# Three more groups' sums turned by VectorE in blocks, and a one-hot moved ahead of each block turn

## The chip, the cores and the metric

The kernel runs on one core of a Trainium2 chip. TensorE (matmuls), VectorE, ScalarE and GpSimd each work through their own queue of instructions in order, and SyncE issues most of the DMAs; between the queues only semaphores order the work. The metric is the device time of one execution in microseconds (us). The profile calls the engines PE (PEld for its weight loads), DVE, ACT, POOL and SP; "q" behind a name is the engine's sequencer.

## The reference

Two graph layers on 1250 nodes of 512 features, with 40000 edges (source, destination, a 512-wide attribute each), sorted by destination:

```
h = relu(layernorm(x))
msg = (h[src] + edge_attr) @ Wm.T + bm
agg = segment_sum(msg, dst) / max(degree, 1)
x1  = x + layernorm(h + gelu(concat(h, agg) @ Wu.T + bu)) * gamma + beta
h1  = relu(layernorm(x1))
rst = (1 + eps) * h1 + segment_sum(h1[src], dst)
out = x1 + relu(rst @ W1 + b1) @ W2 + b2 + h1
```

The kernel sums first and multiplies afterwards: it needs the sum of the edge attributes for each destination (a 1250 x 512 table, kept transposed in `aggT`) and a matrix of counts, how often each source node occurs for each destination (`A16`, 16 bit). With the counts, both sums over `h[src]` become dense matmuls.

## The kernel before

**Groups.** The edges are read in NG = 79 groups of 512, group n by one DMA of 1 MB into buffer n % 4 of `ea` (`sync`, L351 to L357). As destinations are sorted, half a group touches at most W = 22 neighbouring nodes. One step n of the main loop on each engine stands for group n.

**Sums.** `sums(n)` (L1170) is TensorE's work for group n: matmuls with the one-hot `oneD` of destinations as the weights and the edge data moving. VectorE makes that one-hot in `sums_hots(n)` (L725, the instruction is on L729), three groups ahead. The sums come out with destinations on the partitions and must be turned before they can be added to `aggT`. There are two ways, and `EARLY` divides them:

- Groups below EARLY: `sums` writes 8 matmuls of 256 columns (L1185; each is two records in the trace). ScalarE copies them out (`packed_copy`, L512), TensorE turns them with two transposes (`turn`, L1208, the instruction on L1213), ScalarE copies again (`turned_copy`, L518), and GpSimd adds both halves to `aggT` (L445).
- Groups from EARLY on: `sums` writes 16 matmuls of 128 columns (L1193), laid out so that a transposition within blocks of 32 x 32 is enough. VectorE does it straight out of TensorE's memory (`turn_blocks`, L762, the instruction on L768), and adds both halves itself (`add_sums_of`, L770, the instruction on L779). `sums(n)` for n of at least EARLY + 2 waits until `turn_blocks(n - 2)` is done, since both write the same bank (L1177).

**Counts.** The counts are made ahead: `counts(m)` (L1197) on TensorE and `add_counts(m, half)` (L754, L760) on VectorE are done for up to two groups m a step, so that group 78 is counted at step FULL = 58. Step 57 has groups 76 and 77, step 58 has group 78. EARLY is FULL + 1 = 59.

**The handover.** From step 60 on TensorE has one or, from step 64, pairs of "pieces": `piece(i)` (L1276, matmuls on L1295 and L1296) multiplies the 512 x 128 block of `h` in two parts (`Hh`, `Hl`) with a block of the counts. From step 64 the loop takes steps in pairs, both `sums` first. Piece 0 needs all counts added, the block converted by ScalarE (`piece_conv`, L562), the bank free that VectorE empties in `bias_out` (L783, tile `cbB`), and `Hl` from VectorE (`low_h0`, L794), which in turn needs `Hh` from ScalarE (`high_h0`, L551). `high_h0(0)` waits for the bias product (L1149) at the end of TensorE's step 58.

**VectorE's order.** Its program is the loop at L867. In a step n from 60 to 66 it issues: `turn_blocks(n - 1)`, the loading of that group's offsets into registers, `sums_hots(n + 2)`, the two additions of group n - 1, `low_h0(n - 58)`, and one `fold` (L804), a 16-bit addition over 1280 elements toward the degrees. Step 58 has the counts of group 78 and `low_h0(0)`; step 59 has `bias_out`, `low_h0(1)` and two folds; step 67 has a maximum over the degrees (L917) in place of the fold. At step OUT_AT = 70 VectorE waits for piece 9 before it goes on. After the loop TensorE goes on with the update (L1401), the second layer's counts (L1377, L1378) and the two dense layers (L1454, L1470).

Of the kernel before, what the change touches and what calls it, by code (L numbers as in the profile page):

```python
# [18 lines left out]
SUM_HOTS = 3  # L19
# [11 lines left out]
def gnn_kernel(nc, x, src, dst, edge, Wm, bm, Wu, bu, gamma, beta, W1, b1, W2, b2, eps, out):  # L31
# [9 lines left out]
    NG = -(-E // GE)  # L41
    ETAIL = E - (NG - 1) * GE
    GP = NG + 1
    HB = NT
# [7 lines left out]
    NX = NP // XW  # L52
    WU_ORDER = list(range(FC, 2 * FC)) + list(range(FC))
    assert ETAIL % 2 == 0 and ETAIL <= GE // 2 and D == GE and FC == 4 and sum(n for _, n in QS) == NP
    assert len(QS) == 3 and QS[2][1] * 2 == 512 and KW <= 256 and NT == 10

# [5 lines left out]
    FULL = COUNTED.index(NG)  # L62
# [15 lines left out]
    assert all(T_AT[b] + 2 <= U_AT[b][0] for b in range(NT)) and GEN_AT not in ASIDE  # L78

    WARM = 5  # L80
    EARLY = FULL + 1
    FOLD_AT = [EARLY] + list(range(EARLY, EARLY + HB - 2))
    CONV_AT = FULL + 1
    PIECE_AT = FULL + 2
    DEG_AT = FOLD_AT[-1] + 2
    DEG_PARTS = [range(0, NT // 2), range(NT // 2, NT)]
# [4 lines left out]
    IN_LOOP = NG - PIECE_AT  # L91
    assert IN_LOOP <= 2 * NT and HAS_AT[-1] < NG and DEG_AT + 4 < HAS_AT[0] and len(FOLD_AT) == HB - 1
    assert len(BIAS_AT) == NT and all(BIAS_AT[b] <= HAS_AT[b] for b in range(NT))
    PAIRS_FROM = PIECE_AT + 4
    PAIRED = [[n] for n in range(PAIRS_FROM)] + [[n for n in (k, k + 1) if n < NG] for k in range(PAIRS_FROM, NG, 2)]
    assert PAIRS_FROM > max(EARLY, GEN_AT) and [OUT_AT, OUT_AT + 1] in PAIRED
    DEG_BANK = 2
# [119 lines left out]
    with ctx:  # L217
# [198 lines left out]
        def _(pool):  # L416
# [16 lines left out]
            def add_sums_of(n):  # L433
                _, loaded = nc.values_load_multi_w_load_instructions(
                    offrow[0:1, n * 4:n * 4 + 2].bitcast(I32), engines=(mybir.EngineType.Pool,), min_val=0, max_val=(NP << 16) - 1,
                    skip_runtime_bounds_check_because="a pair of least indices of nodes")
                for half, first in enumerate((loaded[0] & 0xFFFF, loaded[0] >> 16)):
                    first = nc.s_assert_within(first, 0, NP - 1, skip_runtime_bounds_check_because="each is the least of indices of nodes")
                    cols = aggT[:, :, bass.ds(first, W)]
                    if half == 0:  # L440
                        pool.wait_ge(turned_out, n + 1)
                    if n > 0 or half > 0:
                        pool.wait_ge(early_step, n * 2 + half)
                    sums = turned_sums[n % TURNS][:].rearrange("p (f q) -> p f q", f=FC)[:, :, half * QUAD:half * QUAD + W]
                    nc.gpsimd.tensor_tensor(cols, sums, cols, ALU.add).then_inc(early_step, 1)  # L445

            pool.wait_ge(offs_in, 16)
            pool.wait_ge(sums_zero, 1)
            for n in range(EARLY):
                add_sums_of(n)  # L450
# [26 lines left out]
        def _(act):  # L477
# [30 lines left out]
            def packed_copy(n):  # L508
                act.wait_ge(sums_done, n + 1)
                if n >= TURNS:  # L510
                    act.wait_ge(turned, n - TURNS + 1)
                nc.scalar.copy(packed_sums[n % TURNS][:], ps[:, n % 2, 0:D // 2]).then_inc(packed_out, 1)  # L512

            def turned_copy(n):
                act.wait_ge(turned, n + 1)
                if n >= TURNS:
                    act.wait_ge(early_step, (n - TURNS + 1) * 2)
                nc.scalar.copy(turned_sums[n % TURNS][:], ps[:, 2 + n % 2, 0:D // 2]).then_inc(turned_out, 1)  # L518
# [14 lines left out]
            def bias_parts_out():  # L533
                act.wait_ge(bm_mm, 1)
                nc.scalar.copy(bm_parts[:], ps[:, ASIDE_BANK["product", FC], :]).then_inc(bm_out, 1)
# [34 lines left out]
            for n in range(NG):  # L570
# [3 lines left out]
                if n - 1 == BIAS_PRODUCT_AT[0]:  # L574
                    bias_parts_out()
                if n < EARLY:
                    packed_copy(n)
                if 0 < n <= EARLY:
                    turned_copy(n - 1)
# [27 lines left out]
            large = act.value_load(most1[0:1, 0:1], min_val=0, max_val=E + P)  # L607
            act.wait_ge(sum_step, 2 * (NG - EARLY))
            act.wait_ge(piece_mm, 2 * NT)
# [68 lines left out]
        def _(dve):  # L678
# [46 lines left out]
            def sums_hots(n):  # L725
                if n >= SUM_HOTS:
                    dve.wait_ge(sums_done, n - SUM_HOTS + 1)
                n1 = idxT["srel"][:, :, n:n + 1].broadcast_to([P, SUB, W])
                V.tensor_tensor(oneD[n % SUM_HOTS][:], iotaF[:, 0:W].rearrange("p (a n) -> p a n", a=1).broadcast_to([P, SUB, W]), n1,  # L729
                                ALU.is_equal).then_inc(hotD_ready, 1)  # L730
# [16 lines left out]
            def offsets(n):  # L747
                _, loaded = nc.values_load_multi_w_load_instructions(
                    offrow[0:1, n * 4:n * 4 + 2].bitcast(I32), engines=(mybir.EngineType.DVE,), min_val=0, max_val=(NP << 16) - 1,
                    skip_runtime_bounds_check_because="a pair of least indices of nodes")  # L750
                return [nc.s_assert_within(first, 0, NP - 1, skip_runtime_bounds_check_because="each is the least of indices of nodes")
                        for first in (loaded[0] & 0xFFFF, loaded[0] >> 16)]
# [9 lines left out]
            def turn_blocks(n):  # L762
                dve.wait_ge(sums_done, n + 1)
                if n < TURNS + EARLY:
                    dve.wait_ge(early_step, (n - TURNS + 1) * 2)
                else:
                    dve.wait_ge(sum_step, (n - TURNS + 1 - EARLY) * 2)
                V.transpose(turned_sums[n % TURNS][:], ps[:, n % 2, 0:D // 2]).then_inc(blocks_turned, 1)  # L768
# [27 lines left out]
            def fold(c):  # L796
                if c > 1:
                    dve.wait_ge(fold_step, c - 1)
                here = A16[:, c, 0:NP]
                if c == 1:  # L800
                    dve.wait_ge(add_step, 2 * NG)
                    dve.wait_ge(u1_mm, NT)
                before = A16[:, 0, 0:NP] if c == 1 else acc[:]
                V.tensor_tensor(Dsum[:] if c == HB - 1 else acc[:], before, here, ALU.add).then_inc(fold_step, 1)  # L804
# [60 lines left out]

            count_first, sum_first = offsets(0), None
            for n in range(NG):  # L867
                if n > EARLY:
                    turn_blocks(n - 1)
                    sum_first = offsets(n - 1)  # L870
                if n > 0 and n - 1 + SUM_HOTS < NG:
                    sums_hots(n - 1 + SUM_HOTS)
                for m in COUNTS[n]:
                    first = count_first
                    add_counts(m, 0, first[0])
# [36 lines left out]
                for c in range(1, HB):  # L912
                    if FOLD_AT[c - 1] == n:
                        fold(c)
                if n == FOLD_AT[-1] + 1:
                    dve.wait_ge(fold_step, HB - 1)
# [190 lines left out]
        def _(pe):  # L1107
# [323 lines left out]
            for _, b in filler:  # L1431
                last = times_A(b, "B")
# [66 lines left out]
```

## Time and profile before

| what | value |
|---|---|
| three executions | median 483.59 us (482.88 to 483.61) |
| the profiled execution | 483.73 us; its span, from the first to the last instruction, 481.9 us |
| TensorE busy | 468.1 us (97% of the span) |
| VectorE busy | 260.6 us (54%) |
| ScalarE, GpSimd busy | 172.0 us (36%), 123.3 us (26%) |
| chain that ended last, by engine | PE 89%, DVE 3%, issue 3%, DMA 2%, all else 1% or less each |
| granted TensorE clock | 1.00 of full speed all through |

The page counts an engine as busy while an instruction of its kind is under way; ends of matmuls are modelled, so the distance from one start to the next tells more than a duration. "Idle before" is the time in which the engine stood still ahead of an instruction, with the instruction that the profile holds to have ended it. The chain that ended last is followed back from the last instruction, at each step to what released it.

### The profile page before, as it was taken

The page shows a single profiled execution, that of the slowest core. Times are in us where ns is not written, and L with a number is a line of the kernel's source. Part 1 is how long each engine was busy: PE and PEld are TensorE (multiplying, and loading weights), DVE is VectorE, ACT ScalarE, POOL GpSimd, SP SyncE. Part 2 cuts the span into 40 slices and gives each one's busy share as a digit, 9 for nine tenths or more (in the row PEclk, how much of TensorE's full clock was granted, in tenths as well). Part 3 has the DMA queues.
Part 4 walks back from the last instruction along what each step waited for, and adds up shares of the span by engine and source line. Part 5 has one row for each costly group of instructions (what it writes and reads, how often), then busy time and mean ns, then how long its engine had stood idle before and what let it go on. Part 6 is the DMA issues. An engine that isn't in the chain of part 4 may idle for free.

```text
span 481.9 us, 9420 instructions
## 1 busy us (share of the span) xinstructions
PE 468.1 (97%) x3313; PEld 282.3 (59%) x3313; DVE 260.6 (54%) x615; ACT 172.0 (36%) x332; POOL 123.3 (26%) x185
## 2 busy tenths in 40 slices
PE   6999999999999999999999999899999999999997
PEld 5555555454555455788765755799744449444445
DVE  4799887778787877997847599822000000011011
ACT  6677642333333337521049387920021213000000
POOL 4016434443343422000000232449980000000000
PEclk9999999999999999999999999999999999999999
DMA  8999999999999999999430111030220000010111
GB/s 280 377 395 407 409 387 387 406 389 403 394 387 402 407 396 382 345 347 339 167 89 22 44 45 40 28 148 1 74 101 0 0 0 1 22 44 23 44 44 38
DMA packets 31832, 98.92 MB, mean 205 GB/s; under 512 B 3686, under 2 KB 4906, under 8 KB 31786
## 3 DMA queue, kind: packets, MB, share of 16 engines
q1 hardware_dynamic: 30570, 97.27, 53.4%
q10 hardware_dynamic: 1216, 1.05, 0.7%
q8 instruction: 27, 0.44, 0.4%
q14 instruction: 19, 0.16, 0.1%
HBM read 95.76 MB, written 2.56 MB: 204 GB/s over the span
## 4 chain that ended last, share of the span: by engine, by line
PE 89%; DVE 3%; issue 3%; DMA 2%; DVEq 1%; ACT 1%; SPq 0%; POOL 0%; ACTq 0%; POOLq 0%
PE ps L1470 14%; PE ps L1454 14%; PE ps L1185 11%; PE ps L1401 7%; PE ps L1234 7%; PE ps L1204 6%; PE ps L1377 4%; PE ps L1378 4%; PE ps L1295 4%; PE ps L1213 4%; PE ps L1296 4%; PE ps L1193 3%; PE ps L1137 3%; DMA WmN<-in_L_gnn_Wm_dram 2%; DVE A L760 1%
## 5 line engine op out<-in xcount | busy, mean ns | idle before, releaser
L445 POOL TENSOR_TENSOR aggT<-turned_sums,aggT 128x88 f32 x118 | 61.3, 520 | 96.7 <-ACT turned_sums L518 83.7
L760 DVE TENSOR_TENSOR A<-ps,A 128x220 f32 x158 | 60.8, 385 | 33.0 <-PE ps L1204 24.1
L1098 DVE TENSOR_TENSOR U<-ps,U 128x512 f32<-128x512 f32 x9 | 6.2, 692 | 122.3 <-PE ps L1470 122.3
L1470 PE MATMUL ps<-W2s,hid 128*128 128x512 f32 (+1 forms) x176 | 68.9, 553 | 0.0
L1454 PE MATMUL ps<-aggT,W1s 128*128 (+1 forms) x192 | 67.3, 513 | 0.0
L1185 PE MATMUL ps<-ea,oneD 128*22 128x256 f32 x944 | 62.6, 383 | 3.1 <-issue 2.8
L1454 PEld LDWEIGHTS ps<-aggT,W1s 128*128 128x128 f32 x192 | 36.4, 190 | 30.7 <-issue 30.6
L1470 PEld LDWEIGHTS ps<-W2s,hid 128*128 128x128 f32 (+1 forms) x176 | 32.6, 185 | 36.0 <-issue 34.5
L1185 PEld LDWEIGHTS ps<-ea,oneD 128*22 128x22 f32 x944 | 23.3, 101 | 50.0 <-issue 25.3
L512 ACT COPY packed_sums<-ps 128x256 f32<-128x256 f32 x59 | 22.0, 372 | 80.7 <-PE ps L1185 80.5
L1377 PE MATMUL ps<-AR,Hh 128*128 128x256 f32 (+2 forms) x160 | 43.8, 310 | 0.0
L1378 PE MATMUL ps<-AR,Hl 128*128 128x256 f32 (+2 forms) x160 | 43.0, 305 | 0.0
L739 DVE TENSOR_TENSOR oneK<-iotaP,P_key 128x1760 bf16<-128x1760 bf16 (+1 forms) x40 | 42.6, 1064 | 0.0
L669 ACT ACTIVATE hid<-ps,b1C 128x512 f32 (+1 forms) x24 | 14.6, 608 | 77.7 <-PE ps L1454 77.7
L1204 PE MATMUL ps<-oneK,oneS 128*128 128x220 bf16 x316 | 40.9, 260 | 0.4 <-DVE A L760 0.4
L1234 PE MATMUL ps<-Wu1T,U 128*128 128x512 f32 x80 | 41.3, 598 | 0.0
L1401 PE MATMUL ps<-CT,aggT 128*128 128x512 f32 x80 | 35.5, 592 | 0.0
L1295 PE MATMUL ps<-ARc,Hh 128*128 128x512 f32 x80 | 32.8, 410 | 0.7 <-DVE Hl L794 0.7
L1204 PEld LDWEIGHTS ps<-oneK,oneS 128*128 128x128 bf16 x316 | 29.9, 97 | 2.8 <-issue 1.0
L1296 PE MATMUL ps<-ARc,Hl 128*128 128x512 f32 x80 | 31.6, 394 | 0.0
L1378 PEld LDWEIGHTS ps<-AR,Hl 128*128 128x128 f32 x160 | 30.2, 189 | 1.7
L1377 PEld LDWEIGHTS ps<-AR,Hh 128*128 128x128 f32 x160 | 30.2, 189 | 1.6
(152 smaller groups left out, 631.5 us busy)
## 6 DMA issues: line engine op xcount, KB each, us to landing
ea<-in_edge_attr_dram SPq DMA_DIRECT2D x78, 1024.0 KB, 8.7
X<-in_x_dram SPq DMA_DIRECT2D x1, 2304.0 KB
xt<-in_x_dram SPq DMA_DIRECT2D x9, 256.0 KB, 2.5
out_dram<-U SPq DMA_DIRECT2D x9, 256.0 KB
W1s<-in_L_gnn_W_dram SPq DMA_DIRECT2D x1, 2048.0 KB, 9.0
W2s<-in_L_gnn_W_dram SPq DMA_DIRECT2D x1, 2048.0 KB, 8.4
Wu2N<-in_L_gnn_Wu_dram ACTq DMA_DIRECT2D x2, 512.0 KB, 4.2
WmN<-in_L_gnn_Wm_dram SPq DMA_DIRECT2D x1, 1024.0 KB, 7.3
```

The costliest lines, as they stand in the source:

```text
L445: nc.gpsimd.tensor_tensor(cols, sums, cols, ALU.add).then_inc(early_step, 1)
L760: V.tensor_tensor(cols, ps[:, 4 + m % 2, half * KW:(half + 1) * KW].rearrange("p (h w) -> p h w", w=W), cols, ALU.add).then_inc(add_step, 1)
L1185: last = T.matmul(to.rearrange("p (c d) -> p c d", c=2), oneD[h][:, g * 2 + j, :], data, start=j == 0, stop=j == 1)
L1204: last = T.matmul(ps[:, 4 + m % 2, (j // 2) * KW:(j // 2 + 1) * KW], sources[:, j // 2, :, j % 2], keys[:, j // 2, :, j % 2], start=j % 2 ...
L1234: quarter = T.matmul(ps[:, ASIDE_BANK["u1", b], :], U[:, b, f * P:(f + 1) * P], Wu1T[:, f, :], start=f == 0, stop=f == FC - 1)
L1295: T.matmul(to, Hh[:, c, rows], here, start=c == 0 and (q < 2 or f % 2 == 0), stop=False)
L1296: last = T.matmul(to, Hl[:, c, rows], here, start=False, stop=c == NT - 1 and (q < 2 or f % 2 == 1))
L1377: T.matmul(to, Hh[:, b, rows], AR[:, b, start:start + cols], start=b == 0 and (cols == 512 or f % 2 == 0), stop=False)
L1378: last = T.matmul(to, Hl[:, b, rows], AR[:, b, start:start + cols], start=False, stop=b == NT - 1 and (cols == 512 or f % 2 == 1))
L1401: last = T.matmul(ps[:, 2 + b % 2, :], aggT[:, f, b * P:(b + 1) * P], CT[:, f, :], start=f == 0, stop=f == FC - 1)
L1454: last = T.matmul(ps[:, CHUNK_BANK[k % 4], 0:cols], W1s[:, f, k * P:(k + 1) * P], aggT[:, f, bass.ds(start, cols)], start=f == 0, stop=f = ...
L1470: last = T.matmul(ps[0:rows, Y_BANK[b + half], 0:cols.stop - cols.start], hid[:, k, b * P:b * P + rows], W2s[:, k, cols], start=k == 0, st ...
```

## The change

Two things are changed. EARLY becomes FULL - 2 = 56, so groups 56, 57 and 58 go by VectorE's block turning and not by ScalarE, TensorE's transposes and GpSimd; FOLD_AT is written with FULL so that it stays [59, 59, 60, ..., 66]. And in VectorE's loop `sums_hots` stands ahead of `turn_blocks` and the loading of offsets, for every step from 57 on.

```
-    EARLY = FULL + 1
-    FOLD_AT = [EARLY] + list(range(EARLY, EARLY + HB - 2))
+    EARLY = FULL - 2
+    FOLD_AT = [FULL + 1] + list(range(FULL + 1, FULL + HB - 1))
...
             for n in range(NG):
+                if n > 0 and n - 1 + SUM_HOTS < NG:
+                    sums_hots(n - 1 + SUM_HOTS)
                 if n > EARLY:
                     turn_blocks(n - 1)
                     sum_first = offsets(n - 1)
-                if n > 0 and n - 1 + SUM_HOTS < NG:
-                    sums_hots(n - 1 + SUM_HOTS)
                 for m in COUNTS[n]:
```

## Rows read from the trace of the kernel before

**Rows 1.** All waits of engine PE from 172 to 250 us: total us, times, longest us

```profile
PE ps L1295 <- DVE Hl L794: 0.7, 1, 0.7
PE ps L1193 <- DVE oneD L729: 0.2, 1, 0.2
```

**Rows 2.** Timeline of PE, steps 58 to 61: start us, us, engine, line, operation

```profile
181.75 1.05 PE L1185 MATMUL ps<-ea,oneD 128*22 128x256 f32 x16
182.73 0.44 PE L1213 MATMUL ps<-ident,packed_sums 128*128 128x128 f32 x2
183.00 0.56 PE L1204 MATMUL ps<-oneK,oneS 128*128 128x220 bf16 x4
...
184.37 1.07 PE L1193 MATMUL ps<-ea,oneD 128*22 128x128 f32 x32
185.37 0.44 PE L1213 MATMUL ps<-ident,packed_sums 128*128 128x128 f32 x2
185.74 1.07 PE L1193 MATMUL ps<-ea,oneD 128*22 128x128 f32 x32
187.51 0.47 PE L1295 MATMUL ps<-ARc,Hh 128*128 128x512 f32 x1 [0.70 <-DVE Hl L794]
...
189.75 1.07 PE L1193 MATMUL ps<-ea,oneD 128*22 128x128 f32 x32
```

**Rows 3.** Timeline of DVE, steps 58 to 60; idle before and its releaser in brackets

```profile
183.78 0.39 DVE L760 TENSOR_TENSOR A<-ps,A 128x220 f32 x1 [0.67 <-PE ps L1204]
184.34 0.39 DVE L760 TENSOR_TENSOR A<-ps,A 128x220 f32 x1 [0.18 <-DVE A L760]
185.12 0.69 DVE L794 TENSOR_TENSOR Hl<-X,Hh 128x512 fp32r<-128x512 f32 x1 [0.39 <-ACT Hh L551]
185.73 0.24 DVE L729 TENSOR_TENSOR oneD<-iotaF,T_srel 128x88 f32<-128x88 f32 x1
185.89 0.68 DVE L783 COPY cbB<-ps 128x512 f32<-128x512 f32 x1
186.77 0.69 DVE L794 TENSOR_TENSOR Hl<-X,Hh 128x512 fp32r<-128x512 f32 x1 [0.19 <-ACT Hh L551]
187.38 1.00 DVE L804 TENSOR_TENSOR acc<-A 128x1280 uint16<-128x1280 uint16 x1
188.41 0.83 DVE L804 TENSOR_TENSOR acc<-acc,A 128x1280 uint16<-128x1280 uint16 x1
189.15 0.44 DVE L768 STREAM_TRANSPOSE turned_sums<-ps 128x256 f32<-128x256 f32 x1
189.52 0.21 DVE L729 TENSOR_TENSOR oneD<-iotaF,T_srel 128x88 f32<-128x88 f32 x1
189.81 0.25 DVE L779 TENSOR_TENSOR aggT<-turned_sums,aggT 128x88 f32 x1
190.24 0.25 DVE L779 TENSOR_TENSOR aggT<-turned_sums,aggT 128x88 f32 x1 [0.18 <-DVE aggT L779]
190.41 0.69 DVE L794 TENSOR_TENSOR Hl<-X,Hh 128x512 fp32r<-128x512 f32 x1
```

**Rows 4.** Timeline of PE, the sums of group 65 and of groups 68 and 69

```profile
200.21 1.07 PE L1193 MATMUL ps<-ea,oneD 128*22 128x128 f32 x32 [0.20 <-DVE oneD L729]
...
210.95 2.00 PE L1193 MATMUL ps<-ea,oneD 128*22 128x128 f32 x64
```

**Rows 5.** Timeline of DVE, the block turns of groups 67 and 77

```profile
211.29 0.44 DVE L768 STREAM_TRANSPOSE turned_sums<-ps 128x256 f32<-128x256 f32 x1
...
240.16 0.44 DVE L768 STREAM_TRANSPOSE turned_sums<-ps 128x256 f32<-128x256 f32 x1
240.82 0.25 DVE L779 TENSOR_TENSOR aggT<-turned_sums,aggT 128x88 f32 x1 [0.21 <-DVE turned_sums L768]
```

**Rows 6.** Timeline of ACT, the second copy of group 58's sums

```profile
185.84 0.37 ACT L518 COPY turned_sums<-ps 128x256 f32<-128x256 f32 x1 [0.75 <-PE ps L1213]
```

**Rows 7.** Timeline of POOL, the last addition of group 58

```profile
187.03 0.67 POOL L445 TENSOR_TENSOR aggT<-turned_sums,aggT 128x88 f32 x1 [0.21 <-POOL aggT L445]
```

## The prediction

> **What bounds the kernel now.** I read the page first: TensorE is busy 97% of the span and makes up 89% of the chain that ended last, so a microsecond off TensorE's queue is worth one, provided that nothing else is late in its place. So the next view is where TensorE waits around the change. From 172 to 250 us the profile knows two waits, both ended by VectorE [rows 1]: 0.7 us ahead of piece 0, and 0.2 us ahead of the sums of group 65 [rows 2, 4]. No DMA is among them. The third view is VectorE's timeline at the same place [rows 3]. In steps 59 to 61 it hardly stands still, and TensorE goes by it: the block turn of group 59 starts at 189.15 and is reported for 0.44, and the sums of group 61, which wait for it by the code, start at 189.75, that is 0.60 after the turn's start. The same distance recurs twice. The turn of group 67 starts at 211.29, so sums 69 may start at 211.89; sums 68 start at 210.95 and the pair takes 2.00 where one group takes 1.07, so TensorE itself is there 0.93 later, at 211.88 [rows 4, 5]. The two are level there, and the 2.00 us for the pair is all work. Between 185 and 212 us VectorE is thus as late as TensorE, or later; only step 70, at which it waits for piece 9 by the code, takes it off the path. From there on the chain is TensorE's nearly without a break.
>
> **The change part by part.**
>
> *Three transposes leave TensorE.* One takes 0.27 us from its start to the next work (182.73 to 183.00) and the last, in step 59, takes 0.37 (185.37 to 185.74): 0.91 us in all. The sums cost the same in both layouts, 0.98 against 1.00 us (181.75 to 182.73, 184.37 to 185.37) [rows 2]. If nothing else were late, this is what the change brings: -0.9 us.
>
> *Six copies leave ScalarE, six additions leave GpSimd.* Nobody waits for these engines here, with one exception: `Hh` of block 1 stands behind the copy at 185.84, which waits for TensorE's last transpose [rows 6], and VectorE idles 0.19 for that `Hh` [rows 3]. It goes.
>
> *Three block turns and six additions come to VectorE.* The prices are in [rows 3]. The next instruction starts some 0.08 before the reported end of the one before it (a turn 0.37, an `Hl` 0.61). From a turn's start to the first addition it is 0.66, to the second 0.43 more, to the next instruction 0.17 more. In steps 57 and 58 this is covered. VectorE idles 0.67 ahead of the counts of group 78 at 183.78, and TensorE delivers these 0.54 earlier, since it is two transposes ahead. The additions of group 56 (0.43 + 0.17), a one-hot (0.16) and the turn of 57 (0.37) make 1.13 us; the one-hot was there before, so 0.97 are new, against 1.21 us of cover less some latency. I let the second count addition start at 184.3, as before. Then follow the additions of group 57 (184.6 and 185.0), and `Hl` of block 0 at 185.15: it was at 185.12 because of an idle 0.39 for its `Hh`, which now comes 0.54 earlier. Up to here the change costs nothing, and this is the last cover.
>
> *Then it costs.* From 185.15: one-hot +0.61 = 185.76; turn of 58 +0.16 = 185.92; additions +0.66 = 186.58 and +0.43 = 187.01; `cbB` +0.17 = 187.18 (before 185.89); `Hl` of block 1 +0.60 = 187.78 (186.77); the first fold +0.61 = 188.39; the second +1.03 = 189.42; one-hot +0.74 = 190.16; turn of 59 +0.16 = 190.32, where it was at 189.15. VectorE is 1.17 us later. What TensorE makes of it: sums 60 may start 0.60 after the turn of 58, at 186.5 and not 185.74. Behind this wait stand sums 60 and everything TensorE has. Piece 0 waits for `cbB` (187.18 + 0.68 + 0.16 = 188.0, before 187.51) and its 2.06 us of work end at 190.1 (187.51 to 189.75 less the wait of about 0.2). Sums 61 wait for the turn of 59: 190.32 + 0.60 = 190.9, against 189.75. The whole saving is used up and 1.17 us are lost.
>
> *The one-hot ahead of the turn, on every step.* Before, the one-hot stood between the turn and the first addition and cost nothing: with it the addition starts 0.66 after the turn (189.15 to 189.81) [rows 3], and without any one-hot there, for group 77, it is 0.66 as well (240.16 to 240.82) [rows 5], since the addition waits for the turn's result. Ahead of the turn it has nothing to hide behind. Its price there isn't in the trace. The nearest rows: from a one-hot to a copy that doesn't depend on it 0.16 (185.73 to 185.89), which I take; from a one-hot to a waiting addition 0.29 (189.52 to 189.81) as the upper end; 0, if the turn's start is set by something else, as the lower. From step 61 to 68 there are 8 more of them, so the turn of 67 is later by 1.17 + 8 x 0.16 = 2.45 us. TensorE was level with it, so sums 69 start 2.45 us later: of this it meets 1.8 at sums 65 (1.17 + 4 x 0.16; the row at 200.21 shows that it waits there) and the rest at sums 69.
>
> *GpSimd beside the folds.* GpSimd's last addition runs from 187.03 to 187.70 and is long [rows 7]; the first fold, begun at 187.38, takes 1.00 us where the second takes 0.83 [rows 3]. With GpSimd done before step 59 I let the first fold lose this: 1.03 becomes 0.85, -0.18 us. The ends are 0 (the fold's own form, it alone reads two blocks of `A16`) and -0.18. The Trainium skill, SBUF — State Buffer, section "Who interferes with whom", says that a VectorE instruction with two inputs in SBUF contends with a GpSimd instruction that reads SBUF, and that whoever starts first holds the shared ports to the end. By that rule the 0.18 is all GpSimd's and the sum is 2.27; without it, if the form sets the fold's time, it is 2.45. The rows fit the rule, but two instructions don't prove it.
>
> *Afterwards.* At step 70 VectorE waits for piece 9 and so comes back into step with TensorE. From step 71 on it has 0.16 more a step, against about a microsecond of slack or more that I take from TensorE's having no wait on it up to 250 us [rows 1]. The later stages all begin with TensorE's or VectorE's last results of the loop, so I pass the loss on in full.
>
> The sum: 1.17 + 1.28 - 0.18 = +2.27 us on the profiled execution's 483.73 us, 486.0 us. That execution lies 0.14 above the median of the three runs, so a median would be near 485.9, which I give.
>
> **The rivals.**
>
> *The one-hot hides after all (0 in place of 0.16 for each of nine).* Then the loss is 2.27 - 9 x 0.16 = +0.8 us, 484.4. For it: the sequencer also loads offsets and handles waits between the instructions, and may set the turn's start anyway. Against it: in steps 60 to 66 the turn starts 0.74 after a fold of 0.83, directly behind it [rows 3], so it is VectorE's own work that sets its start.
>
> *The one-hot costs more (0.29).* Then 2.27 + 9 x 0.13 = +3.4 us, 487.1. For it: the turn has two semaphores to wait for and the copy at 185.89 one.
>
> *TensorE's saving arrives: not slower.* One mechanism: VectorE's new work of step 59 (turn and additions of 58, 1.26 us) finds cover, so that the turn of 59 is in time for piece 0's end. It decides at the turn of 59: it would have to start at 189.15 less 0.9, or 188.3, 2.0 us earlier than I work out. If so the time is 483.6 - 0.9 = 482.7. Against it: every interval in the row of instructions above is one that [rows 3] show without idle time.
>
> *The loss is given back later*, in a wait of TensorE behind 250 us that has a fixed time of its own. The issue share of the chain (3%) is the room for it. Then it is between 484 and 485.
>
> **How the numbers follow.** The forecast, 485.9, with its own range of 484.9 to 486.9, has 0.62. The hidden one-hot has 0.12, the dearer one 0.10, the saving 0.06, the loss given back 0.10. The range that should hold 8 times in 10 leaves out the saving and part of the two others: 484.2 to 487.1. About 0.2% (0.97 us) is what a measurement of this kernel can tell from no change. Faster by more needs the saving and a little luck: 0.04. Within 0.2%, up to 484.56: the hidden one-hot, most of the saving, half of what is given back, 0.18. Slower: 0.78.
>
> **What would show it.** TensorE's timeline should have no L1213 after 177 us, sums 58 at 181.5, and new idle time ahead of sums 60 and 61, ended by VectorE. VectorE's should have turns at 183.3, 185.9 and 190.1 for groups 57 to 59, one-hots straight ahead of each, the turn of group 67 at 213.6, and a first fold of 0.83. The wait at sums 65 should be near 1 us, with a further one at sums 69 of about half a microsecond. If sums 61 start at 190.9 or 190.7 and the end isn't later, the loss was given back behind 250 us. If the turns of 59 and 67 stay 22.14 us apart (211.29 less 189.15), the one-hot is hidden and my 1.28 is wrong. If sums 60 start before 186, the cover of step 58 was larger than I saw.

## The result and the profile after

The changed kernel takes 487.20 us, median of six runs (487.03 to 488.61), against 483.65 us (482.88 to 483.82) before, also six: a ratio of 1.0077, with an interval of 1.0067 to 1.0088. It is slower, as forecast, but by 3.6 us and not by 2.3, and lies just outside the range that ended at 487.1.

The head of the page of the changed kernel, and its chain that ended last by engine:

```profile
span 486.1 us, 9495 instructions
PE 468.8 (96%) x3355; PEld 284.1 (58%) x3355; DVE 262.9 (54%) x624; ACT 169.9 (35%) x326; POOL 120.6 (25%) x179
PE 86%; DVE 6%; issue 4%; DMA 2%; DVEq 2%; ACT 0%; SPq 0%; POOL 0%; ACTq 0%; POOLq 0%
```

VectorE makes up 6% of the chain where it had 3%. This profiled execution took 488.61 us, the longest of the six, and it was already 1.69 us behind the kernel before at 81 us of the span, a stretch in which nothing is changed. A second profile of the same kernel (e4 below) shows no such lead-in: at 81 us it is 0.08 behind. I read the change from that one. Its end is not typical either: its span is 485.4 us where the median is 484.7, because the last output's DMA ended 2.16 us after VectorE's last instruction, and 1.40 before. So I compare starts of instructions in it, and spans by medians. All waits of TensorE from 172 to 250 us in it, where before there were 0.7 and 0.2 us [rows 1]:

```profile
PE ps L1193 <- DVE turned_sums L768: 3.3, 4, 1.6
PE ps L1295 <- issue: 0.6, 1, 0.6
```

The four waits are seen one by one in TensorE's timeline of e4 (start us, us, engine, line, operation, idle time before it and who ended it):

```profile
184.01 1.07 PE L1193 MATMUL ps<-ea,oneD 128*22 128x128 f32 x32
186.67 1.07 PE L1193 MATMUL ps<-ea,oneD 128*22 128x128 f32 x32 [1.59 <-DVE turned_sums L768]
188.37 0.47 PE L1295 MATMUL ps<-ARc,Hh 128*128 128x512 f32 x1 [0.63 <-issue]
...
191.13 1.21 PE L1193 MATMUL ps<-ea,oneD 128*22 128x128 f32 x32 [0.65 <-DVE turned_sums L768]
...
202.13 1.07 PE L1193 MATMUL ps<-ea,oneD 128*22 128x128 f32 x32 [0.59 <-DVE turned_sums L768]
...
214.44 1.07 PE L1193 MATMUL ps<-ea,oneD 128*22 128x128 f32 x32 [0.51 <-DVE turned_sums L768]
```

These are sums 59, sums 60, piece 0 and sums 61, 65 and 69. (For piece 0 the profile names no releaser; by the code it needs the bank that VectorE's copy to `cbB` empties, and it starts 0.10 after that copy's reported end.) Sums 59 start 0.36 earlier than before (184.01 against 184.37), so the transposes' time really is saved on TensorE. Sums 60 start 0.93 later (185.74 before), sums 61 1.38 later (189.75), sums 65 1.92 later (200.21), sums 69 2.56 later (214.44 against 211.88) [rows 2, 4]. TensorE's last matmul is 2.56 us later too: what is lost by sums 69 is lost for good.

VectorE's timeline of e4 over the same steps, to be laid beside [rows 3]:

```profile
184.43 0.39 DVE L760 TENSOR_TENSOR A<-ps,A 128x220 f32 x1 [0.18 <-DVE A L760]
...
185.32 0.68 DVE L794 TENSOR_TENSOR Hl<-X,Hh 128x512 fp32r<-128x512 f32 x1
185.92 0.24 DVE L729 TENSOR_TENSOR oneD<-iotaF,T_srel 128x88 f32<-128x88 f32 x1
186.08 0.44 DVE L768 STREAM_TRANSPOSE turned_sums<-ps 128x256 f32<-128x256 f32 x1
186.74 0.25 DVE L779 TENSOR_TENSOR aggT<-turned_sums,aggT 128x88 f32 x1 [0.21 <-DVE turned_sums L768]
187.17 0.26 DVE L779 TENSOR_TENSOR aggT<-turned_sums,aggT 128x88 f32 x1 [0.18 <-DVE aggT L779]
187.58 0.69 DVE L783 COPY cbB<-ps 128x512 f32<-128x512 f32 x1 [0.15 <-issue]
188.19 0.68 DVE L794 TENSOR_TENSOR Hl<-X,Hh 128x512 fp32r<-128x512 f32 x1
188.78 0.82 DVE L804 TENSOR_TENSOR acc<-A 128x1280 uint16<-128x1280 uint16 x1
189.64 0.82 DVE L804 TENSOR_TENSOR acc<-acc,A 128x1280 uint16<-128x1280 uint16 x1
190.38 0.24 DVE L729 TENSOR_TENSOR oneD<-iotaF,T_srel 128x88 f32<-128x88 f32 x1
190.54 0.44 DVE L768 STREAM_TRANSPOSE turned_sums<-ps 128x256 f32<-128x256 f32 x1
...
213.85 0.44 DVE L768 STREAM_TRANSPOSE turned_sums<-ps 128x256 f32<-128x256 f32 x1
```

It is the forecast's row of instructions in the forecast's order, with hardly an idle moment from 185.3 on. The turn of 59 was forecast at 190.14 with a fast first fold, and stands at 190.54; the turn of 67 was forecast 23.42 us later, and comes 23.31 later. At sums 69 and at TensorE's last matmul this is 2.56 us. By medians the span, from the first to the last instruction, is 484.7 us in both timings of the changed kernel: 2.6 more than the kernel before in e4's timing (482.1), and 2.8 more in the first (there the span before is taken as the median time less 1.80). The time is longer by 3.3 (e4) and 3.6. What is missing, 0.7 us in both, isn't inside the span at all: time less span was 1.80 us and is 2.50.

### The profile page after: what moved, and what is told of

Its sections match the earlier page's. It is cut to its first block, busy times and chain, and to the rows that moved or that the text cites. A ratio compares the mean times of both kernels' runs of the same rounds, so it can differ in the third digit from the quotient of the medians.

```text
span 486.1 us, 9495 instructions
## 1 busy us (share of the span) xinstructions
PE 468.8 (96%) x3355; PEld 284.1 (58%) x3355; DVE 262.9 (54%) x624; ACT 169.9 (35%) x326; POOL 120.6 (25%) x179
## 3 DMA queue, kind: packets, MB, share of 16 engines
HBM read 95.76 MB, written 2.56 MB: 202 GB/s over the span
## 4 chain that ended last, share of the span: by engine, by line
PE 86%; DVE 6%; issue 4%; DMA 2%; DVEq 2%; ACT 0%; SPq 0%; POOL 0%; ACTq 0%; POOLq 0%
PE ps L1470 14%; PE ps L1454 14%; PE ps L1185 11%; PE ps L1401 7%; PE ps L1234 6%; PE ps L1204 6%; PE ps L1377 4%; PE ps L1378 4%; PE ps L1213 4%; PE ps L1295 3%; PE ps L1296 3%; PE ps L1137 3%; PE ps L1193 2%; DMA WmN<-in_L_gnn_Wm_dram 2%; DVE A L760 1%
## 5 line engine op out<-in xcount | busy, mean ns | idle before, releaser
L445 POOL TENSOR_TENSOR aggT<-turned_sums,aggT 128x88 f32 x112 | 58.2, 520 | 92.6 <-ACT turned_sums L518 80.3
L1185 PE MATMUL ps<-ea,oneD 128*22 128x256 f32 x896 | 59.5, 383 | 4.2 <-issue 2.8
L1185 PEld LDWEIGHTS ps<-ea,oneD 128*22 128x22 f32 x896 | 22.2, 101 | 48.5 <-issue 23.9
L512 ACT COPY packed_sums<-ps 128x256 f32<-128x256 f32 x56 | 20.8, 372 | 79.4 <-PE ps L1185 79.4
L1295 PE MATMUL ps<-ARc,Hh 128*128 128x512 f32 x80 | 33.9, 423 | 0.6 <-issue 0.6
L463 POOL TENSOR_TENSOR rs<-ve,mhalf 128x1 f32<-128x1 f32 x10 | 7.5, 750 | 102.0 <-DVE ve L1034 102.0
```

Of the source, the lines that this page charges most:

```text
L1185: last = T.matmul(to.rearrange("p (c d) -> p c d", c=2), oneD[h][:, g * 2 + j, :], data, start=j == 0, stop=j == 1)
L1295: T.matmul(to, Hh[:, c, rows], here, start=c == 0 and (q < 2 or f % 2 == 0), stop=False)
```

## The experiments

In the accounts below "outside" means time less span, by medians of the timed runs, and "packets" are instruction packets of the DMA queues that begin behind the span's end. All kernels were timed beside the kernel before, whose medians lay between 483.78 and 483.89.

| kernel | median us | ratio (interval) | span | outside | packets |
|---|---|---|---|---|---|
| before | 483.8 | | 482.0 | 1.8 | 0 |
| e1 one-hot ahead only | 485.31 | 1.0032 (1.0022 to 1.0041) | 483.6 | 1.77 | 0 |
| e2 three groups only | 485.55 | 1.0034 (1.0022 to 1.0046) | 483.1 | 2.50 | 2 |
| e3 one-hot ahead up to step 59 | 485.66 | 1.0035 (1.0022 to 1.0049) | 483.1 | 2.50 | 2 |
| e4 the change again | 487.23 | 1.0067 (1.0053 to 1.0081) | 484.7 | 2.49 | 2 |
| e5 before, longer TensorE program | 486.30 | 1.0040 (1.0024 to 1.0056) | 484.5 | 1.79 | 0 |
| e6 before, longer VectorE program | 484.15 | 1.0011 (1.0001 to 1.0021) | 482.1 | 2.05 | 1 |
| e7 two groups only | 484.15 | 1.0012 (1.0003 to 1.0021) | 482.4 | 1.80 | 0 |
| e8 before, one fold a step | 483.22 | 0.9988 (0.9979 to 0.9997) | 481.4 | 1.79 | 0 |
| e9 the change, VectorE's program cut | 486.43 | 1.0056 (1.0042 to 1.0070) | 484.2 | 2.23 | 1 |
| e10 one group, eased steps | 482.87 | 0.9981 (0.9972 to 0.9990) | 481.1 | 1.8 | 0 |
| e11 two groups, eased steps | 483.12 | 0.9987 (0.9978 to 0.9996) | 481.3 | 1.8 | 0 |
| e12 as e9, longer ScalarE program | 486.60 | 1.0057 (1.0037 to 1.0076) | 484.4 | 2.22 | 1 |
| e13 as e9, GpSimd's program padded | 486.18 | 1.0048 (1.0030 to 1.0066) | 484.4 | 1.79 | 0 |

### The change in its parts: e1, e2, e3, e4

**e1**, the one-hot ahead of the turn, with groups 56 to 58 on the old way (against the changed kernel):

```
-    EARLY = FULL - 2
+    EARLY = FULL + 1
```

> The kernel before with only the second part of the change: the one-hot ahead of the block turn, groups 56 to 58 as before. Queue theory (each one-hot ahead of a turn costs VectorE 0.16 us from step 60 on, and TensorE waits for VectorE at sums 65 and 69): turns of groups 59 and 67 apart by 22.14 + 1.28 = 23.4 us, sums 69 later by 1.4, time +1.4 us. Rival (the loss comes from the three groups alone, the one-hot is hidden): the turns stay 22.1 apart and the time is that of before within 0.3 us.

It took 1.42 us more (485.31 less 483.89). VectorE's turns of 59 and 67 in e1, and TensorE's sums 65 and 69:

```profile
189.72 0.44 DVE L768 STREAM_TRANSPOSE turned_sums<-ps 128x256 f32<-128x256 f32 x1
...
213.13 0.44 DVE L768 STREAM_TRANSPOSE turned_sums<-ps 128x256 f32<-128x256 f32 x1
```

```profile
201.41 1.07 PE L1193 MATMUL ps<-ea,oneD 128*22 128x128 f32 x32 [0.84 <-DVE turned_sums L768]
...
213.72 1.07 PE L1193 MATMUL ps<-ea,oneD 128*22 128x128 f32 x32 [0.49 <-DVE turned_sums L768]
```

The turns are 23.41 us apart, where they were 22.14 [rows 3, 5]: 1.27 us for eight one-hots, 0.16 each. The one-hot ahead of the turn is fully exposed. Sums 69 start 1.84 later than before; 0.41 of that was there at 170 us already, ahead of everything that differs, so 1.43 are the change's, and so is the time.

**e2**, the three groups on VectorE with the one-hot left behind the turn (against the changed kernel):

```
-                if n > 0 and n - 1 + SUM_HOTS < NG:
-                    sums_hots(n - 1 + SUM_HOTS)
                 if n > EARLY:
                     turn_blocks(n - 1)
                     sum_first = offsets(n - 1)
+                if n > 0 and n - 1 + SUM_HOTS < NG:
+                    sums_hots(n - 1 + SUM_HOTS)
```

> The kernel before with only the first part: groups 56 to 58 turned by VectorE, the one-hot behind the turn as before. Queue theory: sums 60 wait for the turn of 58 (+0.6), sums 61 for that of 59 (+0.6), nothing more is added up to sums 69 since VectorE's step is as before: time +0.6 us, first fold 0.82 us. Rival (the groups carry the loss): +2 us or more.

The first fold and the turns of 59 and 67 in VectorE's timeline of e2:

```profile
188.46 0.82 DVE L804 TENSOR_TENSOR acc<-A 128x1280 uint16<-128x1280 uint16 x1
...
190.06 0.44 DVE L768 STREAM_TRANSPOSE turned_sums<-ps 128x256 f32<-128x256 f32 x1
...
212.09 0.44 DVE L768 STREAM_TRANSPOSE turned_sums<-ps 128x256 f32<-128x256 f32 x1
```

The turns are 22.03 us apart: without the reordering nothing is lost from step 60 on. Sums 61 start at 190.65, 0.90 later than before, and the span is 1.0 longer, where 0.6 was expected; a gap of 0.24 ahead of `cbB`, treated under e7, is the largest part of the difference. The time, however, is 1.66 us longer: this kernel has the extra 0.7 outside as well, and e1 has not. Neither the 0.6 of the queue theory nor the rival's 2 us came.

**e3** kept the one-hot ahead up to step 59 only:

```
-                if n > 0 and n - 1 + SUM_HOTS < NG:
+                if n <= FULL + 1 and n > 0:
                     sums_hots(n - 1 + SUM_HOTS)
                 if n > EARLY:
                     turn_blocks(n - 1)
                     sum_first = offsets(n - 1)
+                if n > FULL + 1 and n - 1 + SUM_HOTS < NG:
+                    sums_hots(n - 1 + SUM_HOTS)
```

> The changed kernel, with the one-hot ahead of the turn in steps 57 to 59 only and behind it from step 60 on. Queue theory: only the 8 later one-hots' 1.28 us go, so sums 69 are later than before by 0.7 to 1.0 us, time +0.9 us. Rival (the order matters in the handover, steps 57 to 59, and not in the steady steps): as the changed kernel, over +2 us.

Span +1.0, outside 2.50: as e2 within 0.1 us. The span is as expected, and the time rose by 1.77 and not by 0.9 because of the outside. **e4** is the changed kernel once more.

> The changed kernel once more, beside the others on one chip. Its handover cost 2.5 us in its first profile (sums 69 at +2.5 once the shift at sums 56 is taken off), while its time rose by 3.5 and its span by 2.8. Theory that the rest is the program's own: again 0.6 to 0.7 us more outside the span than the kernel before, +3.5 us. Rival, chance of the chip or the run: outside as before (1.8 us), time +2.5 us.

It gave the rows shown above, and 487.23 us. The two halves nearly add up: span +1.45 (e1) and +0.95 (e2) against +2.6 together, and the 0.7 outside belongs to the groups.

### The time around the span: e5, e6, e9, e12, e13

The DMA view of the changed kernel's first profile, from the end of its span on:

```profile
DMA packets 2, 0.02 MB, mean 3 GB/s; under 512 B 0, under 2 KB 0, under 8 KB 0
q14 instruction: 2, 0.02, 1.0%
```

The same view of the kernel before has no packet:

```profile
DMA packets 0, 0.00 MB, mean 0 GB/s; under 512 B 0, under 2 KB 0, under 8 KB 0
```

Two instruction packets of 8 KB start 0.98 and 2.26 us behind the end of the span. (Time less span also holds what lies ahead of the first instruction, so it can't be laid beside these two numbers.) The change alters the programs of four engines: by the trace VectorE executes 1233 entries and not 1206 (branches and register work included), TensorE 3713 and not 3674, GpSimd 542 and not 563, ScalarE 522 and not 534. So the first pair of trials lengthened TensorE's and VectorE's programs in the kernel before:

```
+    for _ in range(21):          # e5, behind the last matmul
+        T.matmul(ps[:, 0, 0:1], ident[:], ident[:, 0:1], start=True, stop=True)
```

> The kernel before with 21 matmuls of one column behind TensorE's last matmul, into a bank that nobody reads: about as many more TensorE instructions (42 matmul records and their weight loads) as the changed kernel has. They lie beside the last output's DMA. The time around the span is 1.8 us for the kernel before and 2.5 us wherever groups 56 to 58 go by VectorE. Theory A (it goes with the length of TensorE's program): 2.5 us here, time +0.7. Rival B (it goes with the length of another engine's program, or with what the groups do): 1.8 us, time as before.

```
+    for n in range(27):          # e6, behind VectorE's last addition
+        V.memset(pads[:, n:n + 1], 0.0)
```

> The kernel before with 27 one-column memsets behind VectorE's last addition: as many more VectorE entries as the changed kernel has. Theory B (the time around the span goes with the length of VectorE's program): 2.5 us around the span, time +0.7. Theory A (TensorE's program): 1.8 us, time as before.

e5 left the outside at 1.79 and no packet appeared behind the span; its span grew by 2.5 us, which is the padding's own work: the 21 matmuls run from 478.91 to 485.24, at first 0.22 us each and from 481.8 on, at a granted clock of 0.50, 0.43 each, and so outlast the last output's DMA. TensorE is out. There is one more instruction packet of 16 KB (queue 8) in the last 10 us inside the span in e5 and in every kernel that moves three groups, but e5 and e13 have it with an outside of 1.79, so it isn't the cause either. e6 brought one packet, 1.81 us behind the span, and an outside of 2.05 (1.87 to 2.16), half of what theory B expected, with a span unchanged within 0.1:

```profile
DMA packets 1, 0.01 MB, mean 1 GB/s; under 512 B 0, under 2 KB 0, under 8 KB 0
q14 instruction: 1, 0.01, 0.4%
```

One of the two packets is VectorE's. **e9** goes the other way, from the changed kernel. It leaves out a loop, with the loops inside it, in a branch of VectorE's program that this input doesn't take:

```
     with dve.If(uncovered > 0):
...
-        with dve.Fori(0, NT) as b:
-            ...
```

> The changed kernel, but VectorE's program leaves out the loops of the branch for edges that lie outside their half group's window; these inputs don't take that branch, so what is executed up to the last addition is the same. VectorE's program is about 50 instructions shorter than in the changed kernel and 30 shorter than before. Where the time around the span was 2.5 us, the trace has two packets of instructions (8 KB each, queue 14) after the span's end; where it was 1.8, none; with 27 instructions more on VectorE alone one packet and 2.0. Theory (the end of VectorE's program falls into a further block of instructions, which is fetched only at the end): no packet after the span's end, 1.8 us around it, time 0.7 us below the changed kernel. Rival (the shorter ScalarE and GpSimd programs or the three groups themselves cause it): 2.5 us and two packets again.

One packet is left, 0.97 us behind the span, and the outside is 2.23: neither the theory's 1.8 nor the rival's 2.5. So the theory was half right, and VectorE's program is one of two causes. (The span is 0.5 shorter, and 0.31 of that TensorE gains at 116 us. At 114 us VectorE jumps over that block; it stands idle for 0.93 us there, and in e4 for 1.27.) TensorE being out, the other packet had to belong to ScalarE or GpSimd. e12 and e13 are e9 with one of these programs padded at its end:

```
+    for n in range(12):          # e12
+        nc.scalar.copy(pads[:, n:n + 1], onesF[:])
...
+    for n in range(21):          # e13
+        nc.gpsimd.memset(pads[:, n:n + 1], 0.0)
```

> The changed kernel with VectorE's program shortened (the loops of its branch for edges outside their window left out; these inputs don't take it), and with 12 one-column copies behind ScalarE's last instruction, as many as its program lost by the change. If the remaining packet after the span's end is ScalarE's: none, and 1.8 us around the span. If it is GpSimd's or TensorE's: one packet and 2.2 us.

> The changed kernel with VectorE's program shortened in the same way (the loops of its branch for edges outside their window left out), and with 21 one-column memsets behind GpSimd's last instruction, as many as its program lost. If the remaining packet is GpSimd's: none, and 1.8 us around the span. If it is ScalarE's or TensorE's: one packet and 2.2 us.

e12 changed nothing (2.22, one packet). e13 took the last packet away, and with it 0.43 us outside: that is 1.79, as before. Beside e12, which was timed with it and has the same span of 484.4, it is 0.42 us faster. The DMA view behind its span's end has no packet, as that of the kernel before.

So the second packet is GpSimd's, whose program had become 21 entries shorter, and it goes when the program is given them back. With 0, 1 and 2 packets the outside is 1.8, 2.05 to 2.23, and 2.5 us. That is shown. e7, in between with 1224 entries on VectorE and 549 on GpSimd, has no packet. Why is only inferred, and no run isolates it: an engine's program is fetched in blocks, and an end that falls differently against a block's edge leaves one to be fetched at the very end. The Trainium skill, Runtime: NRT & Kernel Launch, section "Instruction fetch mechanics", says that the sequencer fetches the next block while it executes the current one, that crossing a block's edge is mostly hidden, and that a taken branch to a target outside the window stalls for a fetch. Of fetches within the span this trace shows no price that can be told apart; behind its end one packet more went with 0.25 us (e6) and 0.44 us (e9 and e12 against e13). VectorE's jump at 114 us, 0.34 us dearer with the long block than with the short one, would fit what is said of taken branches, but no packet of queue 14 starts between 98.6 and 117.0 us in e4, so no run here shows that it is a fetch.

### Fewer groups, and the steps eased: e7, e8, e10, e11

**e7** moves groups 57 and 58 alone, with the one-hot behind the turn:

```
-    EARLY = FULL - 2
+    EARLY = FULL - 1
```

> EARLY = FULL - 1: only groups 57 and 58 by VectorE, the one-hot behind the turn. Queue theory: one transpose less is saved than with 56, but one turn and two additions less stand in VectorE's queue: sums 61 at +0.3 to +0.6 against the kernel before, span +0.3 to +0.6. Around the span 1.8 or 2.5: it steps with the program's length, a length in between tells where. Rival (each group costs its third of the loss): span +0.7 or more.

It lost 0.37 us, all in the span, within the expected 0.3 to 0.6. The second addition of group 57 and `cbB` in its VectorE timeline:

```profile
186.47 0.25 DVE L779 TENSOR_TENSOR aggT<-turned_sums,aggT 128x88 f32 x1 [0.18 <-DVE aggT L779]
186.64 0.69 DVE L783 COPY cbB<-ps 128x512 f32<-128x512 f32 x1
```

0.17 us lie between them, as in the forecast. In e4 it is 0.41 (187.17 to 187.58), with the idle time put down to "issue". The gap is in e2, e3 and e4, and not in e7 or e9, in which VectorE's program is laid out otherwise; in e9 the distance is again 0.17 (186.65 to 186.82) though the instructions around it are those of e4. But e9 gains nothing by it at the end: the turn of group 62 stands at 198.02 and its first addition at 199.03, 1.01 us apart where it is 0.65 or 0.66 for the groups around it, and with the shift that each has at 170 us taken off sums 69 are 2.61 later than before in e9 and 2.51 in e4. So such gaps come and go when the program is changed elsewhere, and no run here isolates why.

**e8** goes after the two folds of step 59 in the kernel before:

```
-    FOLD_AT = [EARLY] + list(range(EARLY, EARLY + HB - 2))
+    FOLD_AT = list(range(FULL + 1, FULL + HB))
...
+    DEG_AT = FOLD_AT[-1] + 3
```

> The kernel before (EARLY = FULL + 1, one-hot behind the turn) with one fold a step from 59 to 67 in place of two in step 59, and the products and results of the degrees a pair of steps later. Queue theory: VectorE is 0.85 us earlier at the turn of 59, TensorE's waits at sums 61, 65 and 69 go: sums 69 0.7 us earlier, time -0.7 us. Rival (TensorE's waits for VectorE in the kernel before are not real, they come from the profile's model): time as before, within 0.2 us.

The fold and the turn of 59 in e8:

```profile
187.19 1.00 DVE L804 TENSOR_TENSOR acc<-A 128x1280 uint16<-128x1280 uint16 x1
188.11 0.44 DVE L768 STREAM_TRANSPOSE turned_sums<-ps 128x256 f32<-128x256 f32 x1
```

It is 0.6 us faster than before, and the only wait of TensorE left from 172 to 250 us is the 0.7 ahead of piece 0. So VectorE did hold TensorE up in the kernel before: without the second fold in step 59 sums 65 start 0.79 earlier (199.42 for 200.21), of which 0.19 was there at 170 us and 0.60 is the fold's. The same row settles the fold's price: e8's first fold has GpSimd beside it and takes 1.00; in e2 and e4, without GpSimd, the same instruction takes 0.82.

**e10** puts the pieces together: e8's folds, group 58 alone moved (EARLY = FULL), `cbB` ahead of the additions of its step, and each `low_h0` one step later:

```
+                if n - 1 == BIAS_PRODUCT_AT[1]:
+                    bias_out()
                 if n > EARLY:
...
-                if n - 1 == BIAS_PRODUCT_AT[1]:
-                    bias_out()
                 for b in range(NT):
-                    if HH_AT[b] == n:
+                    if HH_AT[b] + 1 == n:
                         low_h0(b)
```

> Group 58 alone goes by VectorE (EARLY = FULL, one-hot behind the turn), and VectorE's steps 58 to 60 are eased: one fold a step, the copy for the bias ahead of the additions in step 59, each Hl one step later, the degrees a pair of steps later. Queue theory: sums 60 start 0.4 us earlier than before, piece 0 0.4 earlier, no wait at 61, 65 and 69: sums 69 1.2 us earlier, time -1.1 us, 0.4 to 0.6 us below the kernel with the folds alone. Rival (what is gained at step 59 comes back as a wait for the later Hl): time as with the folds alone, -0.6 us or worse.

TensorE's timeline of e10:

```profile
184.58 1.95 PE L1193 MATMUL ps<-ea,oneD 128*22 128x128 f32 x64
187.44 0.48 PE L1295 MATMUL ps<-ARc,Hh 128*128 128x512 f32 x1 [0.91 <-ACT ARc L562]
...
189.47 0.75 PE L1193 MATMUL ps<-ea,oneD 128*22 128x128 f32 x20
```

Sums 59 and 60 run without a break, and sums 61 start 0.28 earlier than before. Piece 0 has a new wait of 0.91, for `piece_conv` on ScalarE, at nearly the old place (187.51 before), which eats most of the saved transpose; most of the gain comes from the fold. Piece 0 was expected 0.4 earlier and the time 1.1 lower. It is the fastest kernel of the study, 0.9 us under the kernel before and 0.35 under e8. **e11** moves groups 57 and 58, and leaves each `low_h0` in its old step.

> Groups 57 and 58 by VectorE (EARLY = FULL - 1, one-hot behind the turn), one fold a step, the copy for the bias ahead of the additions in step 59, the degrees a pair of steps later. Queue theory: sums 60 start 0.3 later (the turn of 58 is still behind Hl), piece 0 0.5 earlier, sums 69 0.9 us earlier, time -0.8 us, where the same two groups without the easing gave +0.4. Rival (the groups themselves cost the time, whatever the order): +0.4 us less what the folds alone give, about -0.2 us.

It gains 0.66 us, 0.25 less than e10. That would fit a second group that costs more on VectorE than it saves on TensorE, but e11 differs from e10 in the place of `low_h0` too, so the group's share isn't shown.

## Why the prediction was off by 1.3 us

**What bounds the kernel: right.** VectorE and TensorE were level from step 59 to 69, and what was put on VectorE there came out at the end. e8 is the test from the other side: one fold of 0.8 us off VectorE in step 59 gave 0.6.

**The cover up to 185.15: nearly right.** The second count addition was let start at 184.3 and started at 184.43; the turn of 58 came at 186.08 for 185.92. This is 0.10 once the shift of 0.06 that e4 brings from earlier steps is taken off.

**"Then it costs": right in kind, 0.24 short.** Of the 0.34 by which the turn of 59 came later than forecast (190.48, shift taken off, for 190.14), 0.10 are those above and 0.24 the gap ahead of `cbB`, which no row of before could show. A part of this was luck made good: from the turn of 59 to that of 67 the forecast was 0.11 too long, since it added the eight one-hots to the 22.14 us of before, and the same row of steps takes only 22.03 in e2. So the turn of 67 was 0.23 later than forecast, and not 0.34.

**The one-hot ahead of the turn: right.** 0.16 each, 1.27 us for eight in e1; e4 has 1.17 against before and 1.28 against e2, where 1.28 was forecast. The two rivals that lived on its price, hidden (0) and dearer (0.29), fall.

**GpSimd beside the folds: right.** 0.82 in every kernel in which GpSimd was done, 1.00 in every one in which it wasn't. The rule of the Trainium skill, SBUF — State Buffer, section "Who interferes with whom", agrees with this trace in who gets in whose way, by those two numbers, and the other explanation, the fold's own form, falls, since the form is the same in all. That the first to start keeps the ports to the end isn't borne out in size: in the kernel before GpSimd's addition ran on for 0.32 us beside the fold, and the fold took 0.18 more (GpSimd's times are rough).

**The wait at sums 65 and 69: right in place.** Near 1 us and half a microsecond were forecast; 0.59 and 0.51 came. What is missing at 65 had been lost at sums 61 already, where TensorE came 0.34 later than forecast, as VectorE did.

**The loss passed on in full: right.** TensorE's last matmul is as late as sums 69, so that rival falls too. So does the one that the saving arrives: the turn of 59 would have had to start at 188.3, and started at 190.54.

**The step that failed: the sum, "+2.27 us on the profiled execution's 483.73 us".** It took over the 1.8 us around the span as they were, a term put at nothing without a reason. Inside the span I forecast 2.27, and 2.5 came at sums 69, 2.6 to 2.8 by the medians of the spans. Outside it I forecast nothing and 0.70 came (2.50 for 1.80), 0.25 with VectorE's longer program (e6) and 0.44 with GpSimd's shorter one (e9 against e13). 2.6 and 0.7 make up the 3.3 us of e4, 2.8 and 0.7 the 3.55 of the first timing; 485.9 would have been 486.6 with the right term for the outside, inside the range. Of the 1.3 us the outside is thus a little over half. The rest is 0.23 of VectorE's queue, as above, and 0.1 (e4's timing) to 0.35 us (the first) that no row shows.

What stays open: which rule sets where a program's end must fall, so that the fetch behind the span could be told beforehand, and what makes the gap ahead of `cbB` and its like. In the first profile of the changed kernel piece 0 ran at the lower clock behind the idle 1.59 us (a granted clock of 0.50 from 190.0 to 193.4 us; its 512-column matmuls were 0.43 apart, in e4, with the same idle time and a clock of 1.00, 0.23); sums 69 wait 0.50 us for VectorE anyway. From 81 us to sums 69 that execution lost 2.48 us (4.17 less 1.69), and e4, without the slow piece, 2.48 as well (2.56 less 0.08), so it isn't part of the loss.

## What to carry to other kernels

Where two engines were level, as here, work moved from one to the other was paid in full at once: compare the new queue's instructions from the last idle moment on, one by one, and look first at what could leave that stretch (here a fold of 0.82 us that nobody waited for; moving it gained 0.6 us, where the change lost 3.6). The one-hot between the turn and its addition was free (0.66 us from one to the other with and without it); ahead of the turn it cost its full 0.16 from start to start. And compare time less span, not the span alone, whenever a change makes an engine's program longer or shorter.

## What the runs showed of the hardware

- The time around the span isn't a constant of a kernel: 1.80 us before, 2.50 after, with two 8 KB instruction packets behind the span's end. Padding VectorE's program by 27 instructions brought one (2.05), and padding GpSimd's back by 21 took one away (2.22 to 1.79): 21 instructions more made that kernel 0.42 us faster (e13 against e12).
- A 16-bit fold of 128 x 1280 on VectorE takes 0.82 us alone (e2, e4) and 1.00 with GpSimd's addition beside it (before, e8).
- Jumping over a block of VectorE's program that isn't taken left VectorE idle for 1.27 us, and for 0.93 with the loops of that block left out (e4 and e9, at 114 us); TensorE gained 0.31 by it.
- A block turn of 128 x 256 takes 0.37 us of VectorE to an independent next instruction, and sums that wait for it start 0.6 us after its start (190.54 to 191.13 in e4, 213.13 to 213.72 in e1).
